# A DCT and a chain of convolutions on one core: the transform's columns move into the statistics' PSUM bank, and GpSimd centres all four batches of the next image

## The reference, cut to what matters

```python
x = x + _L0_conv_ref(_gn(x))             # y = Dh @ gn(x) @ Dw^T, per channel
x = x + _L1_conv_ref(_gn(x), ...)        # six steps of
#   h = relu(gn1(y)); h = conv1([t, h]) + b1
#   h = relu(gn2(h)); h = conv2([t, h]) + b2
#   y = y + dt * gn3(h)
```

## Time and profile before

| | |
|---|---|
| median of 3 runs | 3486.4 us (3483.3 to 3488.0) |
| the profiled execution | 3482.3 us, its span 3480.5 us |
| busy: PE, weight loads, DVE, ACT, POOL | 2990.8, 2537.5, 2720.0, 2449.7, 900.6 us |
| share of the span | 86%, 73%, 78%, 70%, 26% |
| mean granted TensorE clock | 0.944 of full |

### The profile page before, as it was taken

One profiled execution on the slowest core, in us unless ns is written; L12 is line 12 of the kernel. 1 busy time (PEld: TensorE's weight loads), 2 busy tenths in 40 slices (PEclk: granted clock), 3 DMA queues, 4 the chain that ended last, 5 costly groups with the idle time before them and its releaser, 6 DMA issues.

```text
span 3480.5 us, 148009 instructions
## 1 busy us (share of the span) xinstructions
PE 2990.8 (86%) x61684; PEld 2537.5 (73%) x61684; DVE 2720.0 (78%) x6273; ACT 2449.7 (70%) x3819; POOL 900.6 (26%) x1293
## 2 busy tenths in 40 slices
PE   2699988999889998899979998899988999888984
PEld 2577777778777887677767777777777777777873
DVE  6688876888778887788867888688876888768883
ACT  0377777777777777777776777777777777777774
POOL 4133311332123231223212331133311332111111
PEclk9799999999999999999989999999999999999997
DMA  4300133113131230421314113221133113131014
GB/s 89 85 22 21 28 51 96 49 59 87 19 96 56 88 68 3 105 86 49 68 26 118 49 49 67 66 79 49 52 64 96 49 49 93 24 95 58 31 49 112
DMA packets 370208, 217.56 MB, mean 63 GB/s; under 512 B 354544, under 2 KB 354912, under 8 KB 367456
## 3 DMA queue, kind: packets, MB, share of 16 engines
q1 hardware_dynamic: 369504, 207.64, 23.5%
HBM read 104.85 MB, written 77.07 MB: 52 GB/s over the span
## 4 chain that ended last, share of the span: by engine, by line
ACT 25%; issue 22%; DVE 21%; PE 20%; POOL 6%; DMA 3%; SPq 2%; DVEq 1%; POOLq 0%; ACTq 0%
PE cps L1475 14%; ACT z L710 9%; ACT z L678 7%; DVE y L1113 3%; POOL m L558 3%; ACT unread_z L698 3%; ACT hb L709 2%; DVE bnt L1139 2%; ACT ha L709 2%; PE dps L1589 2%; SPq L445 2%; DVE hb L1109 2%; PE dps L1581 2%; DVE ha L1109 1%; DMA y<-xa 1%
## 5 line engine op out<-in xcount | busy, mean ns | idle before, releaser
L1475 PE MATMUL cps<-ha,w 64*64 64x392 f16 (+1 forms) x27648 | 1423.9, 348 | 130.5 <-ACT z L678 99.4
L1475 PEld LDWEIGHTS cps<-ha,w 64*64 64x64 f16 x27648 | 1096.6, 110 | 310.4 <-issue 158.0
L1475 PE MATMUL cps<-hb,w 64*64 64x392 f16 x27648 | 1271.1, 333 | 19.7 <-issue 14.3
L678 ACT ACTIVATE z<-cps,bias_now 128x784 f32<-128x784 f32 (+2 forms) x1056 | 763.2, 739 | 671.7 <-PE cps L1475 663.2
L1475 PEld LDWEIGHTS cps<-hb,w 64*64 64x64 f16 x27648 | 1087.8, 107 | 110.4 <-issue 24.0
L515 POOL TENSOR_TENSOR small<-small,half 128x1 f32<-128x1 f32 x304 | 167.8, 552 | 1692.6 <-DVE small L1013 1030.0
L1109 DVE TENSOR_TENSOR ha<-z,ha 128x784 f16<-128x784 f32 (+2 forms) x384 | 383.0, 997 | 106.2 <-ACT z L710 97.8
L1139 DVE BATCH_NORM_STATS2 bnt<-z 128x6 f32<-128x392 f32 (+1 forms) x768 | 388.7, 549 | 93.4 <-ACT z L678 92.7
L1109 DVE TENSOR_TENSOR hb<-z,hb 128x784 f16<-128x784 f32 (+2 forms) x384 | 374.8, 976 | 86.3 <-ACT z L710 77.5
L1113 DVE SCALAR_TENSOR_TENSOR y<-z,small,y 128x784 f32<-128x784 f32 (+2 forms) x384 | 396.7, 1036 | 0.1
L710 ACT ACTIVATE z<-z,small 128x784 f32<-128x784 f32 (+2 forms) x384 | 395.9, 1031 | 0.0
(11 more groups left out here) (161 smaller groups left out, 2599.8 us busy)
## 6 DMA issues: line engine op xcount, KB each, us to landing
xa<-x_dram SPq DMA_DIRECT2D x128, 196.0 KB, 5.0
y<-xa SPq DMA_DIRECT2D x16, 1568.0 KB, 7.6
y_dram<-y SPq DMA_DIRECT2D x128, 196.0 KB, 4.6
x_dram<-x1s SPq DMA_DIRECT2D x30, 784.0 KB, 5.6
fin<-y_dram SPq DMA_DIRECT2D x30, 784.0 KB, 7.3
xs<-in_x_dram SPq DMA_DIRECT2D x116, 196.0 KB, 4.5
fin<-x_dram SPq DMA_DIRECT2D x28, 784.0 KB, 5.7
out_dram<-fin SPq DMA_DIRECT2D x28, 784.0 KB, 3.7
```

What stands on the lines that cost most here:

```text
L678: return nc.scalar.activation(dst, src, ACT.Identity, bias=bias_now[parts, conv:conv + 1], **more)
L1475: return pe.matmul(dst, w[hin * 64:(hin + 1) * 64, kx, a, wl, :], src[:, :, 0:NA], start=(what == "X" and n == 0), stop=(what == "Y" and n ...
```

## The change

- The rows bursts go into a bank of their own, `tps`, and wait only for ACT's copy of the batch before (`ts_done`), no longer for the add.
- The columns bursts go into the last 448 columns of the statistics' bank `sps`. They wait for the copy (as before), for DVE's read of the statistics Z2 of slot 1 (`stat_read`) and for the add of the batch before (`x1_done`). The statistics Z1 of slot 0 in the next phase 0 wait for the last add.
- The bursts have new places (`DCT_ROUNDS`).
- `normalise_first` is gone from DVE; POOL does batches 0 and 1 ahead of `seam` in phase 3's stretch, and batch 2 behind it.
- ACT does the copy of batch 1 ahead of the first evacuation, that of batch 2 ahead of the state of slot 1, and that of batch 3 behind the second evacuation.
- DVE does add 0 after the update and the first statistics of phase 3, add 1 after `euler(1, 2)`, and add 3 ahead of the last statistics.

```diff
-DCT_ROUNDS = (((1, 0), (1, 9)), ((3, 2), (3, 10)), ((5, 0), (5, 8)), ((6, 4), (8, 0)))
+DCT_ROUNDS = (((1, 0), (3, 0)), ((2, 0), (4, 0)), ((3, 6), (5, 6)), ((5, 0), (7, 0)))
...
-        dps = pb("dps")
+        tps = pb("tps")
         sps = pb("sps")
+        xps = sps[:, BANK - 4 * H:BANK]
...
             # POOL, step
                 if kind == MID:
+                    normalise(HALVES * (g + 1) + s, 0)
                     normalise(HALVES * (g + 1) + s, 1)
+                seam(0, conv_at(g, s, 3), fixes + 2, pows)
+                if kind == MID:
                     normalise(HALVES * (g + 1) + s, 2)
-                seam(0, conv_at(g, s, 3), fixes + 2, pows)
...
             # ACT, step
                 copied(0)
+                copied(1)
                 evacuate(0, 0, s, 3, 0, c)
-                copied(1)
+                copied(2)
                 state_part(1, 0, True)
                 state_part(1, 1, True)
                 evacuate(0, 0, s, 3, 1, c)
-                copied(2)
+                copied(3)
                 state_part(1, 2, True)
                 state_part(1, 3, True)
-                copied(3)
...
             # DVE, step
-                if kind == MID:
-                    normalise_first(hn)
...
-                update(1, lambda: euler(1, 0), (lambda: added(0)) if kind == MID else None)
+                update(1, lambda: euler(1, 0))
                 stats_of(3, 0)
+                added(0)
                 euler(1, 1)
                 split_for(4, 0)
+                euler(1, 2)
                 added(1)
-                euler(1, 2)
...
                 stats_of(3, 2)
+                added(3)
                 stats_of(3, 3)
-                added(3)
...
             # PE
             def dct_columns(b, n, dst):
                 pe.wait_ge(ts_done, n + 2)
+                pe.wait_ge(x1_done, n + 1)
...
                 def rows_of(b):
-                    pe.wait_ge(x1_done, NBATCH * hn + b + 1)
+                    pe.wait_ge(ts_done, NBATCH * hn + b + 1)
...
-                    dct_rows(b, NBATCH * hn + b, dps)
+                    dct_rows(b, NBATCH * hn + b, tps)
+                def columns_of(b):
+                    pe.wait_ge(stat_read, stats_before(g, s, kind) + STATS[kind].index((Z2, 1)) + 2)
+                    dct_columns(b, NBATCH * hn + b, xps)
```

More of the change, by code:

```diff
@@ L572, in normalise @@
                                                    m0[:, 6, CQ + c:CQ + c + 1], ALU.mult, ALU.add)
+                if b == 0:
+                    last.then_inc(xn_first, 1)
+                    pool.wait_ge(xn_first, n - HALVES + 1)
+                    return
                 last.then_inc(xn_done, 1)
@@ L831, in copied @@
                     if kind == MID:
-                        batch_copy(b, NBATCH * hn + b, dps)
+                        batch_copy(b, NBATCH * hn + b, tps)
                 copied(0)
+                copied(1)
                 evacuate(0, 0, s, 3, 0, c)
-                copied(1)
+                copied(2)
                 state_part(1, 0, True)
@@ L1197, in half_post @@
                                         ).then_inc(s_m0, 1)
[L1199 to L1205, removed]
             def half_add(b, n, src, buffers=FIRST):
@@ L1394, in added @@
                             dve.wait_ge(x1_out, 16 * first_place(hn) + 16)
-                        half_add(b, NBATCH * hn + b, dps)
-                update(1, lambda: euler(1, 0), (lambda: added(0)) if kind == MID else None)
+                        half_add(b, NBATCH * hn + b, xps)
+                update(1, lambda: euler(1, 0))
                 stats_of(3, 0)
+                added(0)
                 euler(1, 1)
                 split_for(4, 0)
+                euler(1, 2)
                 added(1)
-                euler(1, 2)
                 split_for(4, 1)
@@ L1606, in _ @@
                             dct_rows(b + 1, n + b + 1, tps0, src)
-                        pe.wait_ge(x1_done, n + b + 1)
                         dct_columns(b, n + b, xps0)
@@ L1636, in rows_of, with first_statistics @@
                         pe.wait_ge(xn_done, (NBATCH - 1) * (hn - HALVES) + b)
-                    dct_rows(b, NBATCH * hn + b, dps)
-                between = {(2, 0): lambda: statistics_of(Z1, 0)}
+                    dct_rows(b, NBATCH * hn + b, tps)
+                def first_statistics():
+                    if kind != LAST_MID and kind != LAST:
+                        pe.wait_ge(x1_done, NBATCH * (hn if kind == MID else HALVES * (g + 2)) + 1)
+                    statistics_of(Z1, 0)
+                def columns_of(b):
+                    pe.wait_ge(stat_read, stats_before(g, s, kind) + STATS[kind].index((Z2, 1)) + 2)
+                    dct_columns(b, NBATCH * hn + b, xps)
+                between = {(2, 0): first_statistics}
                 if kind == FIVE:
@@ L1660, in step @@
                         between[at[0]] = lambda b=b: rows_of(b)
-                        between[at[1]] = lambda b=b: dct_columns(b, NBATCH * hn + b, dps)
+                        between[at[1]] = lambda b=b: columns_of(b)
                 convolve(0, 0, s, 3, conv_at(g, s, 3), sets + 2, between)
```

## The result

The changed kernel takes 3461.3 us (median of five runs, 3457.9 to 3470.4) beside 3488.0 us for the kernel before on the same chip: a ratio of 0.9923, 95% interval 0.990 to 0.9946. So it is faster, by 27 us, where 53 were forecast. Its profiled execution took 3458.9 us, with a span of 3457.1 us, against a span of 3480.5 before: 23.4 us less. The same kernel, run again in a later job, gave a ratio of 0.9951 (0.9933 to 0.9969), which is 17 us. So its gain lies between some 17 and 27 us, and is known no better than that.

What follows compares the result with a forecast made beforehand. PE was held by DCT waits for ACT's copy and DVE's add (121.6 us) and a slow clock. 806.84 - 28 x 26.75 = 57.8, less 4.8 for loads: 53 us; 3482.3 becomes 3429, median 4.1 above: 3433, range 3403 to 3466.

Steps and rivals of the forecast that it cites:

- the forecast case of 3405 to 3449: Whole kernel: the expected outcome around 3433 us, given a chance of 0.77.
- the lock between GpSimd and VectorE: Phase 3 rival: POOL's batch 2 and DVE's products hold each other up, 28 us in all, 3461; chance 0.08.
- the upper bound of the loads: Phases 0 and 1: late loads lose at most 0.8 us a step, 14 us over 3449, so 3463.
- Nothing makes copy 0 earlier: Start of phase 3: ACT's copy 0 keeps its place, so PE's first wait stays, 2.3 us instead of 2.86.
- Phase 3 at full clock: MID steps: a walk through PE's bursts and waits ends phase 3 at +25.9 us, against 27.85 before.
- I count 1.4 of the 1.7: Phase 3 with one clock fall: 1.4 of 1.7 us lost work is seen, giving 27.3 us.
- For 2.3 us I take 6 in 10: Phase 3: the clock falls after the first wait in 6 of 10 steps, averaging 26.75 us.
- The rival with two stretches: Phase 3: the clock falls for two stretches, 28.8 us a phase, time 3482 to 3491; chance 0.05.
- So 0.2 us is lost: Phase 0: later loads, landing at the median 4.5 us, delay the Z1 read; 4.8 us over 24 MID steps.
- a sign of being wrong: Among the signs that would refute the forecast: phases 0 and 1 longer by over a microsecond.
- POOL takes batch 0 ... they end when they ended: Phase 3: POOL's two batches ahead of the seam end as before, batch 2 follows; costed at nothing.
- 2.86 was so in 26 of 28: Kernel before, phase 3: the 2.86 us wait was followed by a stretch at 1.2 GHz in 26 of 28 steps.

Runs made afterwards that it cites:

- experiment 3: Changed kernel with batch 0 of normalise back on VectorE and POOL doing batch 1 ahead of the seam, 2 behind it: 3464.3 us, ratio 0.9934.
- Experiment 5: Changed kernel with ten useless matmuls put in front of PE's wait for copy 0 in phase 3 of each MID step: 3415.8 us, ratio 0.9795.
- experiment 2: Changed kernel with SP's loads of batches 0 to 2 of the next half image ahead of the store of last_add's result: 3459.6 us, ratio 0.9919.
- experiment 7: Changed kernel with the statistics Z2 of slot 1 ahead of the rows burst of batch 1: 3410.7 us, ratio 0.9786.
- experiment 10: Kernel of experiment 9 with the statistics Z2 of slot 1 also put ahead of the rows burst of batch 1: 3354.3 us, ratio 0.9613.
- experiment 6: Kernel before with only ACT's copy of batch 0 moved ahead of the state's last quarter of slot 0: 3430.3 us, ratio 0.9823.
- experiment 4: Changed kernel with ACT's copy of batch 0 moved ahead of the state's last quarter of slot 0: 3388.5 us, ratio 0.9713.
- experiment 8: Changed kernel with both ACT's early copy of batch 0 and SP's loads ahead of the store of last_add's result: 3373.1 us, ratio 0.9671.
- experiment 9: Kernel of experiment 8 with DVE's split of slot 0's last quarter moved behind add 0, and add 2 ahead of split (4, 2): 3346.7 us, ratio 0.9585.

## Why the prediction was right in sign and off in size

Forecast 3433, measured 3461, with the right sign; of 53 us came 27. It lies inside the range, but outside the forecast case of 3405 to 3449: the range reached so far only for the lock between GpSimd and VectorE (3461) and for the upper bound of the loads (3463). That the first of these is the very time measured is chance, since the lock isn't the cause (experiment 3). In the profiled executions it is 53 against 23.4, some 30 us to account for.

- **"Nothing makes copy 0 earlier": right.** 28 waits and 66.5 us, where 28 and about 64 were predicted.
- **Phase 3 at full clock: right.** 26.0 us for the 25.9 of the walk. Columns 3 waited the 0.8 of the walk in two of the seven (0.5 in the others), columns 1 0.4 instead of 0.75.
- **"I count 1.4 of the 1.7": right.** With one slow stretch it takes 27.5 (27.3 predicted), 1.45 above full clock.
- **"For 2.3 us I take 6 in 10": this failed, and it is the first term of the miss.** The clock fell in 21 of 28, and in 5 of them for two stretches, at 29.2 us each. The mean of phase 3 became 27.42 instead of 26.75: 19 us. Of these 10 come of the steps with two stretches (5 x 1.9), 6 of the falls beyond the 16.8 steps that I had counted (4.2 x 1.4), the rest of small misses in the three sizes. The rival with two stretches had the right mechanism and a chance of 0.05 for all steps, where I should have priced it as a share of the steps. Its reason against ("after the first stretch PE is busy") was wrong, and the rows of the kernel before spoke against it already: I had read its clock as one fall a step, but 5 of its 28 phases 3 stand at 0.88 or 0.89 and take 29.5 to 30.7 us. Experiment 5 puts the whole cost of the clock at 40 us, more than the whole gain that was measured.
- **"So 0.2 us is lost" to the loads, 4.8 us: this failed too.** The issue came where predicted (0.4 behind the start of phase 0 for 0.5). The landing took 3.7 to 5.7 us with a median about that used, but a late one costs its lateness while an early one gives nothing back, so a median doesn't price it. Nor was the lateness spread at random: it took over 5 us in ten of the 24 steps, all six with s = 3 among them (5.6 or 5.7). Phases 0 and 1 of the 21 steps took 12.4 us more, 8 over the term, of which 10.6 lie in those ten, and 9.4 fell away in experiment 2. The bound of 0.8 a step was also too low: in the step at 778.38 the two phases took 1.3 us more than in the kernel before, which the prediction had named as a sign of being wrong.
- **Not in the sum at all:** phase 2, 6.7 us more, of which 5 lie in the seven steps with s = 0. A slow stretch reaches into five of these, two before (19 us at half rate for 6). The repeat had 2.5 instead of 5, and the FIVE steps gave 4 back. These I can't tell from scatter.
- **"POOL takes batch 0 ... they end when they ended": wrong, and without cost.** In the step at 819.97 they ended 5.6 us behind the start of phase 3, not 2.6, but what follows the seam is wanted only at X3. Experiment 3 found nothing either way.

The rows of the kernel before that speak on the fourth point: one of the five phases 3 with two slow stretches, and the 6.8 us at 1.2 GHz in it.

```profile
1170.91:1200.37 29.46, 25.70 (x383) 18.93 (x376) 24.94 (x49) 21.18 (x33) 10.10 (x14) 0.88 0.05 18
...
1179.81:1186.64 6.83, 6.83 (x63) 4.68 (x62) 3.45 (x14) 1.11 (x2) 1.61 (x3) 0.50 0.01 4
```

"2.86 was so in 26 of 28" was a misreading too. In two of the 26 the fall came only behind a later wait of 1.6 us for DVE's add, so it is 24 of 28. One of the two, in the phase 3 that starts at 2285.69:

```profile
2304.91 1.03 PE L1581 MATMUL dps<-dct,xn 112*112 112x112 f32 x8 [1.61 <-DVE x1s L1212]
...
2306.21:2309.62 3.41, 3.41 (x39) 2.20 (x28) 3.14 (x5) 3.38 (x5) 0.81 (x2) 0.50 0.02 5
```

## What to carry to other kernels

A wait of PE has two prices, its length and the slow clock that may follow; here the second was the larger, and ten matmuls of nothing in the gap showed it in one run. Before a burst is given a new place, look whether its producer stands needlessly late in another engine's list: one copy moved ahead of two activations gave nearly three times what the change of banks and places did, and made that change worth more as well. When a clock column averages over steps, sort the steps by it first: the share with two slow stretches was there to be read in the profile of the kernel before. Price a load that lands near its deadline by its late cases, not by its median.

## What the runs showed of the hardware that was not expected

**The clock.** In phase 3 TensorE's granted clock fell to 1.2 GHz within 2.2 us of the end of the first wait in 24 of 28 steps where that wait was 2.86 us (2.69 in some), in 19 to 23 of 28 where it was 2.40 (2.25 in some; four runs, of three kernels), in 11 of 28 where it was 1.3 (experiment 7) but in 2 of 28 in experiment 10, where it was 1.3 as well, and in none of 28 where it was 1.2 (experiment 6), of 84 where it was 0.7 (experiments 4, 8 and 9) and of 28 where it was filled but for 0.5. A wait for DVE's add of 1.6 to 1.7 us, later in the phase, was followed by a fall in 2 of 28 in experiment 6, and one of 1.2 in none of 56 in experiments 4 and 8. The same wait of 2.40 us came out both ways, within one run and from one run to the next.

**GpSimd beside VectorE.** POOL's timeline in the step at 819.97:

```profile
818.45 7.11 POOL L574 TENSOR_SCALAR xn<-xs,m 112x112 f32<-112x112 f32 x4 [0.21 <-POOL xn L574]
...
827.69 2.29 POOL L574 TENSOR_SCALAR xn<-xs,m 112x112 f32<-112x112 f32 x4 [0.21 <-POOL ha L552]
```

Four equal instructions took 7.11 us beside DVE's splits, Euler updates and products, and 2.29 where DVE did a single split and stood idle for the rest. DVE hardly paid: two splits of 128x784 took 1.09 and 0.96 us beside them (at 820.73 and 823.56), and one took 0.98 where POOL did short copies only (791.10). No experiment took DVE's work away from beside GpSimd's, so that it is the cause is read from the times alone. The Trainium skill ("SBUF — State Buffer", "Who interferes with whom") says that a VectorE instruction with two SBUF inputs contends with a GpSimd instruction that reads SBUF. The trace agrees in so far as GpSimd's instructions took three times as long beside such work, and adds that here GpSimd bore nearly all of it.
